# A cast moved from VectorE to a transfer, and four partial row maxima merged into one, in a fused two-layer kernel

## The reference

```python
# layer 0
xn = layernorm(x)
s  = scan(h_t = a_t*h_{t-1} + b_t)       # from two projections of xn
g  = silu(ffn0(xn))                      # gate/up/down, hidden 3072
x  = x + s * g
# layer 1
xn = layernorm(x)
q, k, v = split(xn @ W_qkv.T)            # 1024 each, one head
s  = softmax(q*scale @ k.T) @ v
xr, xk = token-shift mixes of xn with the row before
g  = silu(sigmoid(xr@W_r.T) * (relu(xk@W_k.T)**2 @ W_v.T))
x  = x + s * g
```

## Time and profile before

| | us |
|---|---|
| median of 2 runs | 1554.61 |
| lowest, highest | 1553.67, 1555.54 |
| profiled execution | 1556.65 |
| its span, first to last instruction of the slowest core (core 3) | 1555.6 |
| spans of the 8 cores | 1542.5 to 1555.6 |

### The profile page before, as it was taken

The page is one execution under the profiler, slowest core; times in us unless marked ns, Lnnn a source line. Parts: engine busy times, 40 slices in busy tenths (PEclk is TensorE's granted clock), DMA queues, the critical chain, the costliest instruction groups (busy, mean ns, idle before and its releaser), DMA issues.

```text
span 1555.6 us, 16796 instructions; the slowest of 8 cores (1542.5 to 1555.6 us)
## 1 busy us (share of the span) xinstructions
PE 1283.8 (83%) x6016; PEld 576.5 (37%) x6016; DVE 503.3 (32%) x543; ACT 375.4 (24%) x420; POOL 140.6 (9%) x236
## 2 busy tenths in 40 slices
PE   1587789999999999997135778889899879888886
PEld 0133334444444444443012333333344434444443
DVE  0614231000112135464387833133331122333232
ACT  1222311111111132332112444222201222222322
POOL 0001111010111100001000000000000102111111
PEclk9798999999999999999568899999999989999998
DMA  8343334237455545643724323623222203333332
GB/s 177 86 77 54 51 59 70 45 70 115 70 80 79 87 97 152 163 118 85 182 81 109 85 64 75 169 57 79 59 37 35 61 15 96 94 92 85 82 75 61
DMA packets 74161, 133.30 MB, mean 86 GB/s; under 512 B 23904, under 2 KB 32096, under 8 KB 72032
## 3 DMA queue, kind: packets, MB, share of 16 engines
q0 software_dynamic: 32384, 77.61, 28.8%
q1 hardware_dynamic: 33632, 42.03, 8.8%
q10 hardware_dynamic: 8064, 12.59, 2.5%
HBM read 159.47 MB, written 29.36 MB: 121 GB/s over the span
## 4 chain that ended last, share of the span: by engine, by line
PE 70%; DVE 15%; ACT 6%; DMA 4%; issue 3%; DVEq 1%; SPq 0%; ACTq 0%; POOL 0%; POOLq 0%
PE psf L347 10%; PE psf L353 10%; DVE BP L145 8%; PE psf L973 7%; PE psf L827 7%; PE psf L468 7%; PE psf L941 7%; DVE FP L145 7%; PE psf L386 5%; PE psf L438 5%; ACT BP L145 4%; PE psf L754 2%; PE psf L766 2%; PE psf L675 2%; PE psf L210 1%
## 5 line engine op out<-in xcount | busy, mean ns | idle before, releaser
L145 ACT ACTIVATE BP<-psf 128x512 bf16<-128x512 f32 (+1 forms) x208 | 144.7, 696 | 634.3 <-PE psf L353 309.5
L347 PE MATMUL psf<-BP 128*128 128x512 bf16 x768 | 187.6, 389 | 30.8 <-DVE BP L145 26.6
L145 DVE TENSOR_TENSOR BP<-BP,psf 128x512 bf16<-128x512 bf16 x96 | 66.0, 688 | 372.4 <-ACT BP L145 371.7
L353 PE MATMUL psf<-BP 128*128 128x512 bf16 x768 | 183.8, 383 | 0.0
L210 PE MATMUL psf<-BP,ones 128*128 128x512 bf16 x64 | 36.1, 563 | 117.1 <-ACT BP L145 105.4
L347 PEld LDWEIGHTS psf<-BP 128*128 128x128 bf16 x768 | 75.4, 99 | 128.0 <-issue 44.0
L973 PE MATMUL psf<-BP 128*128 128x512 bf16 x512 | 115.7, 385 | 2.3 <-ACT BP L145 2.3
L827 PE MATMUL psf<-BP 128*128 128x512 bf16 x512 | 113.4, 383 | 3.8 <-DVE FP L145 3.8
L468 PE MATMUL psf<-BP 128*128 128x512 bf16 x512 | 111.8, 379 | 0.0
L353 PEld LDWEIGHTS psf<-BP 128*128 128x128 bf16 x768 | 75.9, 99 | 93.3 <-issue 4.6
L941 PE MATMUL psf<-BP 128*128 128x512 bf16 x448 | 109.1, 405 | 1.5 <-DVE BP L145 1.2
(11 more groups left out here) (69 smaller groups left out, 1065.1 us busy)
## 6 DMA issues: line engine op xcount, KB each, us to landing
BP<-wg POOLq DMA_DIRECT2D x48, 256.0 KB, 4.5
BP<-wu POOLq DMA_DIRECT2D x48, 256.0 KB, 5.3
BP<-wd POOLq DMA_DIRECT2D x16, 768.0 KB, 8.8
FP<-xt SPq DMA_DIRECT2D x32, 256.0 KB, 8.7
FP<-xt SPq DMA_DIRECT2D x8, 1024.0 KB, 10.0
x1s<-FP SPq DMA_DIRECT2D x8, 1024.0 KB, 8.2
FP<-x1s SPq DMA_DIRECT2D x32, 256.0 KB, 7.8
FP<-x1s POOLq DMA_DIRECT2D x16, 512.0 KB, 6.7
```

The source lines that it names most:

```text
L145: ins = fn(*a, **k)
L347: te.matmul(pg, lhsT, rhs, start=(k == 0), stop=(k == NCH - 1))
L353: ins = te.matmul(pu, lhsT, rhs, start=(k == 0), stop=(k == NCH - 1))
```

## The change

Two edits. In layer 1's normalisation only, the bf16 copy is no longer a DVE instruction but one transfer from SBUF to SBUF on POOL's queue, which casts on the way (2 MB of f32 read, 1 MB of bf16 written). POOL takes the two waits that DVE had, and PE gets one wait more, on the transfer's own counter `s_cs`. In attention, the four partial maxima and the maximum over them become one maximum over 128x2048, issued after the last matmul of the tile.

```diff
@@ CSMM
-                wt(ve, s_ln[par])
-                wt(ve, s_t, st["castuse"].get(sp - 1, 0))
-                vx.tensor_copy(xb0f, xsf)
+                if src_x1:
+                    wt(gp, s_ln[par])
+                    wt(gp, s_t, st["castuse"].get(sp - 1, 0))
+                    inc(gp.dma_start(xb0f, xsf), s_cs, 16)
+                else:
+                    wt(ve, s_ln[par])
+                    wt(ve, s_t, st["castuse"].get(sp - 1, 0))
+                    vx.tensor_copy(xb0f, xsf)
                 wt(se, s_ln[par])
                 wt(se, s_t, st["castuse"].get(sp - 1, 0))
                 sx.activation(sqf, xsf, AF.Square)
                 wt(te, s_s)
                 wt(te, s_v)
+                if src_x1:
+                    wt(te, s_cs)
@@ at_CD
-            mxp = FP[:, F_MISC + par * 8 + 4: F_MISC + par * 8 + 8]
-            for k in range(NCH - 1):
+            for k in range(NCH):
                 lhsT = qt[:, k * 128:(k + 1) * 128]
                 for sps in range(4):
                     rhs = BP[:, R1 + k * T + sps * 512: R1 + k * T + sps * 512 + 512]
-                    te.matmul(psc[:, sps * 512: sps * 512 + 512], lhsT, rhs,
-                              start=(k == 0), stop=False)
-            k = NCH - 1
-            lhsT = qt[:, k * 128:(k + 1) * 128]
-            for sps in range(4):
-                rhs = BP[:, R1 + k * T + sps * 512: R1 + k * T + sps * 512 + 512]
-                ins = te.matmul(psc[:, sps * 512: sps * 512 + 512], lhsT, rhs,
-                                start=False, stop=True)
-                inc(ins, s_t)
-                wt(ve, s_t)
-                vx.reduce_max(mxp[:, sps:sps + 1],
-                              psc[:, sps * 512:(sps + 1) * 512], axis=AX.X)
+                    ins = te.matmul(psc[:, sps * 512: sps * 512 + 512], lhsT, rhs,
+                                    start=(k == 0), stop=(k == NCH - 1))
+            inc(ins, s_t)
             qt_free[par] = s_t.n
+            wt(ve, s_t)
             wt(ve, s_s, mx_free[par])
-            vx.reduce_max(mx, mxp, axis=AX.X)
+            vx.reduce_max(mx, psc, axis=AX.X)
             vx.tensor_scalar(bias, mx, -QSCALE, None, ALU.mult)
```

More of the change, by code:

```diff
@@ L121, in build_program @@
     s_qw = mksem("s_qw")
+    s_cs = mksem("s_cs")
     def inc(instr, sem, k=1):
```

## The result

The changed kernel is 0.6% slower: the ratio of its time to that of the kernel before is 1.0059, with a 95% interval of 1.0044 to 1.0075, which is 9.2 us (6.8 to 11.7) of 1555.5. The forecast was 2.9 us. The profiled execution took 1560.19 us, among the shortest of its kernel.

A forecast was written before the change was run, and what follows sets the result against it. The prediction took PE's matmuls to bound the kernel, with DVE edits counting only where PE waits for DVE. It summed +5.7 - 2.4 - 0.4 = +2.9 us, from 1554.61 to 1557.5 us, range 1552 to 1564 us.

The forecast's parts named there:

- Span 0: Start of layer 1's normalisation: PE waits for the transfer, landing 9.55 us after issue, and nothing covers it; +5.7 us.
- the straight line through the weight loads: Transfer time for 1024 KB, extended from the best landing times of 256 KB and 768 KB casting weight loads; 9.55 us.
- Span 1: Layer 1's normalisation: PE starts about 0.2 us later, but DVE needs the sums only after the mixes; cost 0.
- Span 2: Layer 1's normalisation: the transfer is done ahead of need, so PE no longer waits for DVE's copy; -2.4 us.
- Span 3: Layer 1's normalisation: the transfer, behind the `wk` loads, lands before PE's start, which waits for ACT's square; cost 0.
- Edit 2: Attention's single maximum of 2.29 us: only the first tile's wait gets shorter, later tiles hide it; -0.4 us.
- Rival 2: Slow transfer, 20.6 us to landing, costing time in spans 0 and 3; +16.4 us in total, 1571 us; chance 0.12.

The follow-up runs named there:

- c11: Changed kernel with layer 1's load of span 1 held back until the transfer of span 0 has landed; ratio 1.0023 to the kernel before.
- c4: Changed kernel with the transfer in span 2 alone, the copies of spans 0, 1 and 3 back on DVE; ratio 0.9974 to the kernel before.
- c8: c4 with PE's sums of span 2 waiting only for what they read, not all of DVE's work; ratio 0.9928 to the kernel before.
- c3: Changed kernel with the copy of span 3 back on DVE, spans 0, 1 and 2 by transfer; ratio 1.0020 to the kernel before.
- c2: Kernel before with the single maximum in attention only, the copy still on DVE; ratio 0.9999 to the kernel before.
- c5: Changed kernel with the transfer of span 3 cut into eight of 512 columns on the same queue; ratio 1.0022 to the kernel before.
- c6: Changed kernel with four staging slots instead of two for the q projection's stores; ratio 1.0051 to the kernel before.

## Why the prediction was wrong

The direction was right, and most of the steps. The size was 2.9 us where 9.2 were measured, 6.3 us too little. The median of all runs, 1565.16 us, lies above the range of 1552 to 1564; the base of the forecast and the measured change, 1554.61 + 9.2 = 1563.8 us, reach its upper edge. By the prediction's own steps:

- **Span 0, forecast +5.7 us, measured +6.85.** The term had the right mechanism. L from issue to landing was 9.4 us on core 3, against 9.55 from the straight line through the weight loads. The other cores needed up to 2.0 us more, and POOL takes up its work 0.4 us after ACT does (760.36 against 759.94), which the sum left out. The reason that I gave for the value was wrong, though: "in span 0 it starts when the loads are nearly drained". The loads of span 1 were not drained, and c11 puts their share at 3.2 us. The transfer alone is quicker than the line says; two errors cancelled, and that L came out right on core 3 is luck. The other reason, that the eight cores share HBM, is tested by no run here. The transfer of span 1, which no load shared, landed in 6.9 us:

```profile
BP<-FP POOLq DMA_DIRECT2D x1, 1024.0 KB, 6.9
```

By the fixed cost and rate of the Trainium skill ("DMA: Bandwidth & Descriptors", section "Anatomy of one DMA — SWDGE (gpsimd) path") the prediction had estimated 6.8 us for it; for a transfer that is alone the trace agrees.

- **Span 1, forecast 0.** Right: DVE finds its sums done after the mixes.
- **Span 2, forecast -2.4 us, measured -2.0, and -2.3 in c4.** Right, and DVE's wait for the sums stayed (5.84 us). I noted that PE waits for all of `s_v`, and took it as given. c8 shows that narrowing it takes 5.3 us more out of the stage than c4 does (214.7 to 209.4), twice what moving the cast gives.
- **Span 3, forecast "Cost: 0, with a cover of 18.2 us". This step failed.** It asked when the transfer's result is needed, and there the answer was right: it landed 8.8 us after its issue, long before the sums, and PE waited for ACT's square as before. It put at nothing what the transfer does to others, and did not ask who else uses the DMA engines during those 8.8 us. I had written that "POOL's queue loses nothing", and looked at that queue alone. ACT's stores lie on another queue and share the same engines. Their 2.0 us to landing was in the trace, as was the fact that ACT waits for them (14.1 us in ten waits before, the longest 2.6), and with two slots ACT had no room for a store of 6.8 us. c3 prices the omission at 6.1 us in time, and at 7.15 us in the projection or 5.4 in the normalisation. The forecast was 6.3 us short.
- **Edit 2, forecast -0.4 us.** Its size holds in the first tile (15.59 to 15.19), and c2 is consistent with it, but can't tell it from nothing. The length of 2.29 us for the maximum was exact.
- **Rival 2** reached the measured region, 1564 to 1571 us, by a slow transfer. That was not the mechanism: the transfers took 6.9 to 11.4 us over all spans and cores. The sentence on what would make me wrong names a transfer over 13 us, a longer DVE operation and a late L1031, and none of the three happened.

What stays open is why hardly a packet of the stores is served in the first 4 us, when later the queues go packet for packet. c5 shows that smaller pieces help, not whether their size or their spacing does it.

## What to carry to other kernels

A transfer that is done long before anyone needs it can still cost something while it runs: list every other queue's transfers in that window, the time that each has to spare and the number of slots behind it. When work is moved off a busy engine, look first at which wait ends last in that stretch: here a wait on a whole counter, where one value of it would have done, was worth more than the moved work. And a stop of PE can cost more than its length, since PE may run at the lower clock behind it; 4.08 us of standing brought 2.90 us more.

## What the runs showed that I had not expected

A casting transfer within SBUF is a dense load: 1 MB written in 6.9 us alone, 9.4 to 11.4 us beside eight loads of 256 KB. Beside it, stores of 128 KB took 6.8 us to land instead of 2.0. PE, after a stop of 4.08 us, ran for 5.84 us at a granted clock of 0.50, the level of 1.2 GHz, and before the stop it had been busy at the full clock for 7.10 us; after a stop of 0.67 us in c6 its 16 matmuls took the 3.61 us of the full clock (1.00), and after one of 2.13 us on core 3 of c6 it ran for 3.14 us at 0.54.
